# Score masks of a language-model tower issued as 32x128 tiles instead of 32x64 tiles

## The reference, cut to what matters

```python
i = jnp.arange(W)[:, None]                 # W = 64 queries of a block
j = jnp.arange(2 * W)[None, :]             # the block before, then the own block
base = (j > i) & (j <= i + W)
blk0 = (jnp.arange(nb) > 0)[:, None, None] | (j >= W)[None, :, :]
mask = base[None, :, :] & blk0
sc = jnp.where(mask[None, None], sc, -jnp.inf)
p = jax.nn.softmax(sc, axis=-1)
...
lmask = jnp.arange(N_LATENTS)[None, :] <= (jnp.arange(Sx) // chunk)[:, None]
lsc = jnp.where(lmask[None, None], lsc, -jnp.inf)
```

## Time and profile before

| | |
|---|---|
| median of 3 runs | 2922.24 us (2906.99 to 2924.91) |
| the profiled execution's own time | 2924.72 us |
| its span, first to last instruction | 2922.7 us |
| TensorE busy / weight loads busy | 91% / 64% of the span |
| VectorE / ScalarE / GpSimd busy | 59% / 42% / 33% |
| mean granted TensorE clock | 0.963 |

### The profile page before, as it was taken

How to read it: one execution, slowest core, us unless ns; L and a number is a source line. 1 busy time by engine, 2 the same in 40 slices (tenths; PEclk the granted TensorE clock), 3 DMA queues, 4 the chain that set the end, 5 groups by cost and what they waited for, 6 DMA issues and landing times. The chain is left out here.

```text
span 2922.7 us, 109244 instructions
## 1 busy us (share of the span) xinstructions
PE 2667.8 (91%) x47656; PEld 1862.1 (64%) x47656; DVE 1737.8 (59%) x5573; ACT 1233.5 (42%) x2659; POOL 967.7 (33%) x1417
## 2 busy tenths in 40 slices
PE   2799999999999999999999997169999999999998
PEld 1566677767767767677676676136666666666665
DVE  3466666666656666566665654766667575675700
ACT  0444444544444445454444542034434334344342
POOL 2323323323323324233233220024353443434433
PEclk9899999999999999999999998579999999999999
DMA  2000001000000000000000000101121112211120
GB/s 65 19 22 24 24 22 26 25 24 23 24 24 23 24 24 26 22 24 24 23 26 22 24 19 14 35 26 40 57 69 32 66 32 69 66 37 64 33 69 28
DMA packets 58915, 98.31 MB, mean 34 GB/s; under 512 B 12124, under 2 KB 43816, under 8 KB 58440
## 3 DMA queue, kind: packets, MB, share of 16 engines
q0 software_dynamic: 18624, 51.14, 6.2%
q1 hardware_dynamic: 39816, 40.17, 4.2%
HBM read 55.88 MB, written 33.82 MB: 31 GB/s over the span
## 5 line engine op out<-in xcount | busy, mean ns | idle before, releaser
L895 PE MATMUL banks<-hT,w 128*128 128x512 f32 x1024 | 468.6, 605 | 11.0 <-ACT hT L712 10.9
L1160 DVE TENSOR_REDUCE mx<-banks 128x8 f32<-128x1024 f32 x256 | 301.3, 1219 | 150.5 <-PE banks L1003 150.5
L686 ACT ACTIVATE probT<-banks 128x1024 f32<-128x1024 f32 x256 | 259.8, 1028 | 231.9 <-PE banks L1046 231.9
L723 ACT ACTIVATE hid<-banks,b 128x512 f32<-128x512 f32 x256 | 176.3, 689 | 399.0 <-PE banks L895 399.0
L532 POOL TENSOR_TENSOR h<-ve,mhalf 128x2 f32<-128x2 f32 x128 | 92.0, 719 | 737.1 <-DVE ve L1201 737.1
L895 PEld LDWEIGHTS banks<-hT,w 128*128 128x128 f32 x1024 | 187.6, 192 | 213.0 <-issue 197.3
L510 POOL DMA_INDIRECT rows<-in_tok_table,idx_now x132 | 138.5, 1049 | 475.3 <-DVE hres L1138 390.1
L1059 PEld LDWEIGHTS V_ps<-Ve,probT 128*64 128x64 f32 x4096 | 257.7, 141 | 34.4 <-issue 34.2
L1059 PE MATMUL V_ps<-Ve,probT 128*64 128x17 f32 x4096 | 271.4, 213 | 4.9 <-issue 4.9
L1059 PE MATMUL V_ps<-Vo,probT 128*64 128x17 f32 x4096 | 271.8, 213 | 2.2 <-issue 2.2
L1235 DVE TENSOR_SCALAR_CACHE_REDUCE hits<-act_s,cval 128x128 bf16<-128x128 f32 x960 | 261.2, 343 | 2.3
(11 more groups left out here) (223 smaller groups left out, 5566.2 us busy)
## 6 DMA issues: line engine op xcount, KB each, us to landing
h_rows<-h SPq DMA_DIRECT2D x128, 130.0 KB, 2.0
w<-in_w SPq DMA_DIRECT2D x16, 1024.0 KB, 5.3
Qt<-low SPq DMA_DIRECT2D x512, 2.0 KB
Gq<-lowl SPq DMA_DIRECT2D x256, 2.0 KB
rows<-in_tok_table,idx_now POOLq DMA_INDIRECT x132, 3.5
out_rows<-orow,idx_cur POOLq DMA_INDIRECT x128, 2.5
b<-in_b SPq DMA_DIRECT2D x8, 128.0 KB, 4.5
hrow<-h_rows,idx_next POOLq DMA_INDIRECT x64, 2.8
```

Source lines behind the costliest of these rows:

```text
L686: nc.scalar.activation(dst[:, 2 * pair:2 * pair + 2, :], banks[:, 2 * pair:2 * pair + 2, :], ACT.Exp).then_inc(s_exp, 1)
L723: nc.scalar.activation(hid[:, m, :], S_ps[m % 2][:, 0:GT * P], ACT.Gelu_apprx_tanh, bias=b1[:, m:m + 1]).then_inc(s_hid, 1)
L895: mm = nc.tensor.matmul(S_ps[m % 2][:, 0:GT * P], w1[:, c, m * P:(m + 1) * P], hT[g % 2][:, c, :], start=c == 0, stop=c == KC - 1)
L1160: nc.vector.tensor_reduce(tops.rearrange("p (g h) -> p g h", g=2), banks[:, 2 * pair:2 * pair + 2, :].rearrange("p g (h k) -> p g h k", h= ...
```

## The change

The masks' stationary operands become 128 columns wide, so that a mask matmul writes both sides (all 128 partitions) of a bank at once.

- By query, latents: 4 matmuls of 512 columns where there were 8.
- By query, local, units 2 to 4: 8 matmuls of 512 columns where there were 16. Unit 1, whose first half has no block before it, takes 16 of 256 columns: the block before and the own block go separately, and the first one's table blots out the first half.
- By key, latents: 8 of 512 columns where there were 16.
- By key, local: the side of the queries chooses the stationary table, and all four use one moving table of 64 keys. 16 matmuls of 256 columns where there were 16 of 512. The block before has the opposite mask of the own block: a constant row (row 0, -1e30 throughout) plus the own block's row times minus one.

The scores stay as they were, at 32 rows and 64 columns.

```diff
+    hot = (r == i % W).astype(np.float32)
+    first_hot = np.where(i < W, r == W - 1, hot)
+    by_query = np.concatenate([np.where(q <= r, NEG, 0.0), np.where(q > r, NEG, 0.0)], 2)
+    by_key = np.where((r > q) | (r == 0), NEG, 0.0)
+    diag_key = np.where(r == 0, 0.0, r == q)
+    none_key = np.broadcast_to(r == 0, diag_key.shape)
+    prev_key = none_key - diag_key
+    even_queries = np.concatenate([diag_key, prev_key], 2)
+    first_queries = np.concatenate([diag_key, none_key], 2)
+    odd_queries = np.concatenate([prev_key, diag_key], 2)
...
                     for g in range(G):
-                        for a in range(2):
-                            nc.tensor.matmul(banks[side[a], g, :].rearrange("p (j t n) -> p j t n", j=2, t=TS),
-                                             ownhot[strip[g], side[a]],
...
+                        nc.tensor.matmul(banks[:, g, :].rearrange("p (j t n) -> p j t n", j=2, t=TS),
+                                         ownhot[strip[g], :],
...
                 for r in range(2):
-                    for g in range(G):
-                        for a in range(2):
-                            nc.tensor.matmul(banks[side[a], g, :].rearrange("p (h k) -> p h k", h=G), onehot[strip[g], r, :],
-                                             by_query[strip[g], min(t, 1) if a == 0 else 1, r, :].unsqueeze(1)
-                                             .to_broadcast([32, G, P]), start=r == 0, stop=False)
+                    if t == 0:
+                        for first, cols in ((True, side[0]), (False, side[1])):
+                            for g in range(G):
+                                nc.tensor.matmul(banks[:, g, :].rearrange("p (h k) -> p h k", h=G)[:, :, cols],
+                                                 (first_hot if first else hot)[strip[g], r, :],
+                                                 by_query[strip[g], r, cols].unsqueeze(1).to_broadcast([32, G, W]),
+                                                 start=r == 0 and first, stop=False)
+                    else:
+                        for g in range(G):
+                            nc.tensor.matmul(banks[:, g, :].rearrange("p (h k) -> p h k", h=G), hot[strip[g], r, :],
+                                             by_query[strip[g], r, :].unsqueeze(1).to_broadcast([32, G, P]),
+                                             start=r == 0, stop=False)
...
                 for r in range(2):
-                    for g in range(G):
-                        for a in range(2):
-                            if u == 0:
-                                nc.tensor.matmul(banks[side[a], g, :], onehot[strip[g], r, :], lat_key[strip[g], r, :],
-                                                 start=r == 0, stop=False)
-                            else:
-                                keys = odd_key[strip[g], min(t, 1), r, :] if a else even_key[strip[g], r, :]
-                                nc.tensor.matmul(banks[side[a], g, :].rearrange("p (h k) -> p h k", h=G),
-                                                 onehot[strip[g], r, :], keys.unsqueeze(1).to_broadcast([32, G, P]),
-                                                 start=r == 0, stop=False)
+                    if u == 0:
+                        for g in range(G):
+                            nc.tensor.matmul(banks[:, g, :], hot[strip[g], r, :], lat_key[strip[g], r, :],
+                                             start=r == 0, stop=False)
+                    else:
+                        for keys, cols in ((even_queries if t else first_queries, side[0]), (odd_queries, side[1])):
+                            for g in range(G):
+                                nc.tensor.matmul(banks[:, g, :].rearrange("p (h k) -> p h k", h=G)[:, :, cols],
+                                                 keys[strip[g], r, :],
+                                                 by_key[strip[g], r, :].unsqueeze(1).to_broadcast([32, G, W]),
+                                                 start=r == 0 and cols == side[0], stop=False)
```

More of the change, by code:

```diff
@@ L71, in constants @@
     rows = 32 * np.arange(2)[None, :] + (i % 32)[:, None]
-    onehot = rows[:, :, None] == q[None, None, :]
     r = rows[:, :, None]
[L74 to L79, removed]
+    hot = (r == i % W).astype(np.float32)
[8 more added lines that the diff above has]
+    odd_queries = np.concatenate([prev_key, diag_key], 2)
     step = S // NL
@@ L86, in constants @@
     cols = [f(ident), f(parity * HD ** -0.5), f(parity), f(parity * (NL / S)), f(unit), f(before), f(lane), f(i),
-            packed(onehot), packed(own), packed(by_query), packed(even_key), packed(odd_key), packed(lat_query), packed(lat_key)]
+            packed(hot), packed(first_hot), packed(own), packed(by_query), packed(by_key), packed(even_queries), packed(first_queries),
+            packed(odd_queries), packed(lat_query), packed(lat_key)]
     digit = np.arange(1, RADIX, dtype=np.int64)[None, :] << (32 - BITS * (1 + np.arange(DIGITS, dtype=np.int64)))[:, None]
@@ L129, in tower @@
         at = np.cumsum([0] + widths)
-        (c_ident, c_query, c_parity, c_latent, c_unit, c_before, c_lane, c_part, onehot, ownhot, by_query, even_key, odd_key,
-         lat_query, lat_key) = (cst[:, int(at[n]):int(at[n + 1])] for n in range(len(widths)))
-        onehot = onehot.bitcast(BF16).rearrange("p (r m) -> p r m", r=2)
+        (c_ident, c_query, c_parity, c_latent, c_unit, c_before, c_lane, c_part, hot, first_hot, ownhot, by_query, by_key,
+         even_queries, first_queries, odd_queries, lat_query, lat_key) = (cst[:, int(at[n]):int(at[n + 1])] for n in range(len(widths)))
+        hot, first_hot, by_query, by_key, even_queries, first_queries, odd_queries = (
+            a.bitcast(BF16).rearrange("p (r k) -> p r k", r=2)
+            for a in (hot, first_hot, by_query, by_key, even_queries, first_queries, odd_queries))
         ownhot = ownhot.bitcast(BF16)
-        by_query = by_query.bitcast(BF16).rearrange("p (v r k) -> p v r k", v=2, r=2)
-        even_key = even_key.bitcast(BF16).rearrange("p (r q) -> p r q", r=2)
-        odd_key = odd_key.bitcast(BF16).rearrange("p (v r q) -> p v r q", v=2, r=2)
         lat_query = lat_query.bitcast(BF16).rearrange("p (t n) -> p t n", t=TS)
@@ L974, in top_scores @@
                     for g in range(G):
-                        for a in range(2):
-                            nc.tensor.matmul(banks[side[a], g, :].rearrange("p (j t n) -> p j t n", j=2, t=TS),
-                                             ownhot[strip[g], side[a]],
-                                             lat_query[strip[g], :, :].unsqueeze(1).to_broadcast([32, 2, TS, NL]),
-                                             start=True, stop=False)
+                        nc.tensor.matmul(banks[:, g, :].rearrange("p (j t n) -> p j t n", j=2, t=TS),
+                                         ownhot[strip[g], :],
+                                         lat_query[strip[g], :, :].unsqueeze(1).to_broadcast([32, 2, TS, NL]),
+                                         start=True, stop=False)
                     for n in range(2 * TS):
```

## The result

The changed kernel takes 2935.0 us, the median of 20 runs, against 2916.6 us in 20 runs of the kernel before: a ratio of 1.0066 (95% interval 1.0046 to 1.0086), by which it is 19 us slower. The forecast was 2959 us, 37 us slower: the direction is right and the time lies in the range, but the size is twice what was measured, and a slowdown beyond 1% did not come.

A forecast was written before the change was run, and what follows sets the result against it. It took TensorE, busy 97% of full attention stretches, as the bound. 320 batches x 0.12 us made 38 us, 95% of it 36.5, with tables 37: 2922.2 + 37 = 2959 us, range 2919 to 2980 us.

The forecast's parts named there:

- The seam: From 32x128 mask to 32x64 scores: shape change 0.10 us plus first weights 0.02 us, 0.12 us in each of 320 batches.
- The emptying: Between mask and scores, TensorE drains at the change of shape: 0.10 us a batch, bounds 0 and 0.15.
- the scores' first weights: At the start of the scores, weights that cannot be loaded ahead: 0.02 us a batch, bounds 0 and 0.05.
- The change into 32\*128: Ahead of each mask, rows change from 128 to 32 either way, so its 0.10 us stays and nothing is added.
- rounds of 256 columns: Within the masks, rounds should lie 0.107 to 0.11 us apart; 0.15 or more would mean weight loads bound them.
- rival 3: In the masks, wider weight loads do not hide behind 256-column rounds: up to 47 us more, 2980 to 3006 us; chance 0.05.
- rival 1: At the start of the scores, no seam between 32x128 and 32x64: 2912 to 2923 us, most likely 2920; chance 0.17.
- The step that failed: In the mask batches, half the matmuls of 160 batches go but the same columns stream: costed at nothing.
- 95% of the added time: In the attention stage, waits for work not hanging on TensorE absorb a little: 38 us added becomes 36.5 us.
- Rival 2: In the attention stage, the seam is there but half goes into slack: 18 us left, 2940 us; chance 0.08.

The follow-up runs named there:

- experiment 5: Kernel before with 32x128 masks by query alone, the 512-column ones cut in two of 256, putting 896 matmuls and weight loads back: ratio 1.0023 to the kernel before.
- experiment 4: Kernel before with some 512-column masks cut in two of 256, no new seam, 1152 matmuls and weight loads more: ratio 1.0056 to the kernel before.
- experiment 8: Kernel before with unit 0 (latents) by query wholly in 32x128, masks and scores: ratio 0.9898 to the kernel before.
- experiment 10: Changed kernel with the latents' scores by query in 32x128 as well, its other 288 seams kept: ratio 0.9975 to the kernel before.
- experiment 6: Kernel before with the experts' first matmul cut in two of 256 columns, 1024 matmuls and weight loads more: ratio 1.0010 to the kernel before.
- experiment 1: Changed kernel with its 512-column masks cut in two of 256, putting 1152 matmuls and weight loads back: ratio 1.0082 to the kernel before.

## Why the prediction was half right

**The seam** was sized a little low. Taken from starts, as medians over all batches, from a mask's first matmul to the first of the next task:

| batches | before, us | after, us | a batch |
|---|---|---|---|
| 32 latents by query | 1.715 | 1.849 | 0.134 |
| 32 unit 1 by query | 1.549 | 1.701 | 0.152 |
| 96 units 2 to 4 by query | 1.549 | 1.685 | 0.136 |
| 32 latents by key | 1.430 | 1.588 | 0.158 |
| 128 local by key, the fastest | 1.852 | 1.994 | 0.142 |
| the same, medians of units 1, 2, 3, 4 | 1.895, 1.880, 1.887, 1.853 | 2.250, 1.998, 2.086, 2.017 | 0.355, 0.118, 0.199, 0.164 |

With the fastest by key the sum is 45 us, where the prediction had 320 x 0.12 = 38; with the medians by key it is 54 us. The 9 us between them come late in the scores by key, with no idle time above 0.15 us, and their cause is open. The emptying is 0.09 us, near the 0.10 of the earlier trace rows. By the Trainium skill ("TensorEngine Tiling (Array Packing)", Key Properties) a change of tiling mode drains TensorE; these 0.09 us agree, for two shapes of 32 rows. The rest of the seam is the scores' first weights, 0.05 us and not the 0.02 of the earlier trace rows: the second round of scores starts 0.16 us after the first, before 0.11. The change into 32\*128 cost nothing new, and rounds of 256 columns lie 0.11 to 0.12 us apart, so neither rival 3 nor rival 1 came about.

**The step that failed** is this one: "Half the matmuls of 160 batches go, but nothing that is streamed. Costed at nothing: the array was streaming meanwhile." The array was, but the program was not free. The batches are 54 us longer and the kernel 19 us, so 35 us came back. In the profiles the idle time by issue falls by 28 us, and over all runs the mean granted clock rises from 0.963 to 0.967, some 12 us of full clock over the span (an estimate). That the time still lies in the range is luck: the seams were sized 16 us too low, and the relief was left out. 896 of the 1152 matmuls, put back at the same seams, cost 23 us (experiment 5); 1152 added without a seam cost 16 us (experiment 4). The prediction had the sign of its evidence before it: the largest of the waits in the earlier trace rows is 16.4 us of L985 for "issue", 12 times up to 2.1 us, in a run with no semaphore inside. I read the named waits only, and asked of that row neither what it waits for nor what it does to the clock.

**Waits.** "I take 95% of the added time as reaching the end" was near the truth for what it meant: the waits for other engines, 34 us before, gave back some 5 of the 54 us. Rival 2 of the prediction gives about the measured time, 18 us, for the wrong reason: the slack that took the time up was TensorE's own.

**How the parts add up.** Three parts can be read for every kernel: the longer medians of its batches (in experiment 4 of those without a stop), the idle time by issue of its profile, and the clock that was not granted (1 - granted clock, times the span, the mean of all runs). Their sum against the kernel before is an estimate of the difference: for the change 54 - 28 - 12 = +14 us (measured +19), by query alone 22 - 27 - 13 = -18 (-16), in experiment 4 2 + 16 + 2 = +20 (+16), in experiment 8 11 - 28 - 21 = -38 (-30), in experiment 10 61 - 39 - 29 = -7 (-7). It fits worst by key alone, 32 - 6 - 10 = +16 (+8), and in experiment 6, 0 - 6 - 3 = -9 (+3).

**What it does not settle.** The relief has two sources that do not add: fewer dense instructions (experiments 4, 5) and the pauses at the seams (experiment 1: same number, 24 us where the batches say 54). Whether a seam is paid in full once most stops are gone is not shown: masks by key on top of masks by query cost 1.0066 - 0.9944 = 1.2% or 36 us, where their batches say 32, and alone 0.3%; but the change on top of wide latents costs 0.9975 - 0.9898 = 0.8% or 23 us, where its batches say 50. Why some runs of the same instructions stop and others do not, and why some stops are followed by the low clock and others not, stays open.

## What to carry to other kernels

Count instructions for each microsecond of the busiest engine, and look at its idle time by "issue" in the middle of a run: where it stands there, thinning out the densest run can pay even if that run gets longer (30 us here). A change of tile shape within an accumulation cost a seam of about 0.14 us here; change the shape where it changes anyway, or give masks and scores the same one. Eight narrow tiles that already streamed at a column a cycle (0.22 us for 512 columns) gained nothing here from being four wide ones but a shorter program.

## What was not expected of the hardware

TensorE can wait for its own program: here it went on 1.2 to 1.6 us after a block of 256 instructions had landed. Each of the 11 stretches at the lower clock between 150 and 1750 us of the kernel before begins right behind such a stop, of 0.5 to 2.1 us; at 1538 us the 1.38 us idle were followed by some 10 us at 0.50. But of the 21 stops of 0.8 us or more only 9 are followed by one. And a matmul more with its weight load costs 0.014 to 0.026 us where they stand densely (16 us for 1152, 23 us for 896), and nothing measurable where each lasts 0.2 us.
